# Causal attention in a Macaron block: masking inside VectorE's maximum instruction, whole-array maximum products in one even order, y turned a quad later

## What is computed

```python
def pair_attention_mask(t):
    m = jnp.tril(jnp.ones((t, t), dtype=bool))
    odd = jnp.arange(1, t, 2)
    return m.at[odd, odd - 1].set(False)
...
scores = jnp.einsum('bhqd,bhkd->bhqk', q, k) * scale
mask = pair_attention_mask(t)
scores = jnp.where(mask, scores, -jnp.inf)
w = jax.nn.softmax(scores, axis=-1)
y = jnp.einsum('bhqk,bhkd->bhqd', w, v)
```

## Time and profile before

| | us |
|---|---|
| median of 3 runs | 2261.66 (2257.74 to 2266.56) |
| the profiled execution | 2277.73 |
| its span, first to last instruction | 2275.9 |
| stage of the change in it | 1238 to 1818, 580 |
| busy in the span: PE, DVE, ACT, POOL | 1893.5, 1707.0, 1007.7, 799.4 |

### The profile page before, as it was taken

How to read it: one execution, slowest core, us unless ns; L and a number is a source line. 1 busy time by engine, 2 the same in 40 slices (tenths; PEclk the granted TensorE clock), 3 DMA queues, 4 the chain that set the end, 5 groups by cost and what they waited for, 6 DMA issues and landing times. The chain is left out here.

```text
span 2275.9 us, 37061 instructions
## 1 busy us (share of the span) xinstructions
PE 1893.5 (83%) x11875; PEld 1340.2 (59%) x11875; DVE 1707.0 (75%) x3526; ACT 1007.7 (44%) x1972; POOL 799.4 (35%) x862
## 2 busy tenths in 40 slices
PE   2799997799997369889797799999999874588898
PEld 1677787687775257778674233333333362477787
DVE  8789874688886666768887777777777366676688
ACT  1333435333334523335565355555555635233345
POOL 2223321233333667773346000000000036677733
PEclk9999997999998669999998799999999986699999
DMA  5000001000002512234347254353342016122246
GB/s 181 1 1 0 0 1 35 22 1 0 0 1 77 184 47 86 87 89 146 105 117 173 39 71 56 51 71 56 51 71 37 1 56 206 40 87 89 87 138 194
DMA packets 116656, 156.61 MB, mean 69 GB/s; under 512 B 20967, under 2 KB 85773, under 8 KB 115981
## 3 DMA queue, kind: packets, MB, share of 16 engines
q1 hardware_dynamic: 99840, 112.83, 21.4%
q0 software_dynamic: 14400, 40.41, 5.7%
q10 hardware_dynamic: 2252, 1.29, 0.2%
HBM read 107.00 MB, written 47.20 MB: 68 GB/s over the span
## 5 line engine op out<-in xcount | busy, mean ns | idle before, releaser
L2083 DVE TENSOR_REDUCE t_nm<-ps 128x1 f32<-128x512 f32 (+3 forms) x768 | 390.5, 552 | 102.3 <-PE ps L2173 50.7
L2149 ACT ACTIVATE t_E<-ps 128x1024 f32<-128x1024 f32 (+3 forms) x384 | 295.1, 808 | 244.4 <-PE ps L2201 191.1
L1569 PE MATMUL ps<-m_w,m_xT 128*128 (+1 forms) x1248 | 347.9, 414 | 10.3 <-DVE m_xT L1649 9.0
L1569 PEld LDWEIGHTS ps<-m_w,m_xT 128*128 128x128 f32 x1248 | 223.2, 192 | 53.2 <-issue 14.9
L693 PE MATMUL ps<-wdT,f_hT 128*128 128x256 f32 (+1 forms) x768 | 194.8, 396 | 18.2 <-ACT f_hT L735 18.2
L2198 PE MATMUL ps<-t_Qs,t_Ks 98*128 98x512 bf16 (+3 forms) x768 | 198.6, 339 | 5.0 <-DMA t_Qs<-t_mT 3.9
L1587 PE MATMUL ps<-m_w,m_hT 128*128 (+1 forms) x1248 | 201.5, 297 | 0.5 <-DVE m_hT L1666 0.5
L1656 DVE TENSOR_TENSOR m_ab<-ps,m_b 128x512 f32<-128x512 f32 x208 | 142.4, 685 | 68.5 <-PE ps L1569 45.2
L2068 POOL COPY t_Va<-t_V 128x128 f32<-128x128 f32 x64 | 16.1, 295 | 487.0 <-DVE t_mp L2094 486.8
L192 POOL TENSOR_TENSOR f_h<-f_h,f_hs 128x704 f32<-128x704 f32 x64 | 88.7, 1386 | 276.2 <-DVE f_h L230 276.2
L1621 ACT ACTIVATE m_hT<-ps 128x256 fp32r<-128x256 f32 x208 | 79.9, 384 | 223.5 <-PE ps L1578 135.2
(11 more groups left out here) (299 smaller groups left out, 3975.4 us busy)
## 6 DMA issues: line engine op xcount, KB each, us to landing
m_raw<-in_L_ffn_rw SPq DMA_DIRECT2D x48, 256.0 KB, 3.2
t_parts<-t_qkv_part SPq DMA_DIRECT2D x64, 192.0 KB, 2.8
t_Qs<-t_parts SPq DMA_DIRECT2D x96, 128.0 KB, 4.1
t_Ks<-t_parts SPq DMA_DIRECT2D x96, 128.0 KB, 6.7
m_yl<-m_picked_out SPq DMA_DIRECT2D x40, 256.0 KB, 2.9
m_rows<-m_xn SPq DMA_DIRECT2D x16, 512.0 KB, 4.2
m_xg<-m_rows SPq DMA_DIRECT2D x64, 128.0 KB
m_y<-m_picked_out SPq DMA_DIRECT2D x24, 256.0 KB, 3.1
```

The lines of the kernel that those rows point to most:

```text
L1569: last = nc.tensor.matmul(ps[:, H1 + u, :], xT[:, u, kx, k, :], of_expert(w1, kw, e, k), start=n == 0, stop=n == 3 * DC - 1)
L2083: nc.vector.tensor_reduce(dst, ps[:, bank, 0:n], AX_X, ALU.max, negate=True).then_inc(emptied, 1)
L2149: nc.scalar.activation(E[:, s % NPB, :, 0:n], ps[:, bank:bank + 2, 0:n], ACT.Exp, scale=float(HD) ** -0.5).then_inc(e_ok, 1)
```

## The change

- The maximum product is one for each head, on 96 rows of `Qs` and `Ks` from all six products of parts. `Qo` and `Ko` and their six transfers a quad go. The mask products at L2173 go.
- On the diagonal VectorE's instruction is `tensor_tensor_reduce`: it adds a bf16 row (`forbidden`: zeros, and the mask in the last 128 columns), multiplies by -1, takes the minimum into an accumulator, and writes the elementwise result to `unread`, which nothing reads.
- The 48 products go from large to small over the heads. `spread` places them over slots in proportion to the columns of TensorE's other work, without a break over the quads: those of quad q+1 end at slot 17 of quad q, and those of q+2 begin at slot 18. Each slot has two places, ahead of its scores and behind them. `nm` and `nm2` are double.
- `turn_max` for q+1 comes at slot 19 of quad q, y0 of q at slot 13. The last value products of a quad and its y1 come in the next quad, at slots 1 and 3.
- `y_ok` is dropped; ScalarE and SyncE wait for `pv_ok`.

```diff
--- before.py
+++ after.py
@@ -1921,49 +1921,85 @@
...
     QB = TPB
-    MAX_STEPS = [(pair, qb, k0, min(512, (qb + 1) * P - k0)) for pair in range(2) for qb in range(QB)
+    MAX_STEPS = [(h, qb, k0, min(512, (qb + 1) * P - k0)) for qb in reversed(range(QB)) for h in range(QUAD)
...
+    MAX_BY, M_AT, Y0_AT, Y1_AT = 18, 19, 13, 3
...
+    def columns(s):
+        Q, kb, _ = EXP_SLOTS[s]
+        n = 512 - max(0, kb - 4 * Q) * P
+        return 2 * n + (2 * P if kb >= 4 * Q else 0), (4 * n + 512 if s % 2 else 0)
+    def spread(slots):
+        places = [(s, i) for s in slots for i in range(2)]
+        work = [columns(s % NE)[i] for s, i in places]
+        share, at = sum(n for _, _, _, n in MAX_STEPS) / sum(work), {p: [] for p in places}
+        p, room = 0, work[0] * share
+        for k, (_, _, _, n) in enumerate(MAX_STEPS):
+            while room < n / 2 and p + 1 < len(places):
+                p += 1
+                room += work[p] * share
+            at[places[p]].append(k)
+            room -= n
+        return at
+    OF_FIRST, OF_REST = spread(range(MAX_BY)), spread(range(MAX_BY - NE, MAX_BY))
+    def max_steps(q, s, i):
+        steps = []
+        for j in (q + 1, q + 2):
+            if j < QUADS:
+                steps += [(j, k) for k in (OF_FIRST if j == 1 else OF_REST).get((s - (j - q - 1) * NE, i), ())]
...
+        at = {}
+        def put(*what):
+            at[what] = len(at)
+        for k in range(NM):
+            put(0, k)
+        put(0, "m")
+        for q in range(QUADS):
+            for s in range(NE):
+                for i in range(2):
+                    for j, k in max_steps(q, s, i):
+                        put(j, k)
+                if s == Y1_AT and q:
+                    put(q - 1, "y1")
+                if s == Y0_AT:
+                    put(q, "y0")
+                if s == M_AT and q + 1 < QUADS:
+                    put(q + 1, "m")
+        put(QUADS - 1, "y1")
+        return at
...
-            side, r = divmod(i - 2 * len(QPARTS), 3)
+            side, r = divmod(i, len(QPARTS))
             rows = scratch[side][q:q + 1, (QPARTS, KPARTS)[side][r], :, :]
-            odd = rows.rearrange("q (g o p) t -> p (q g) o t", o=2, p=HD)[:, :, 1, :]
-            sp.dma_start((Qo, Ko)[side][c][SECOND + r * HD:SECOND + (r + 1) * HD, :, :], odd).then_inc(stacked[c], 16)
+            sp.dma_start((Qs, Ks)[side][c][r * HD:(r + 1) * HD, :, :],
+                         rows.rearrange("q (h p) t -> p (q h) t", p=HD)).then_inc(stacked[c], 16)
...
         yT = ch.sb(name + "yT", [P, 512], ctx=until_y_done)
+        forbidden = ch.sb(name + "forbidden", [P, 512], BF16, ctx=until_y_done)
+        unread = ch.sb(name + "unread", [P, RING, 512], BF16, ctx=until_y_done)
...
                     if not end:
-                        sp.wait_ge(y_ok, q * 2 + 1)
+                        sp.wait_ge(pv_ok, q * NE + 4)
                         sp.sem_inc(ch.fence, 1)
                         stack(q + 2, (c + 2) % NQ)
...
-                        dst = (nm if k0 == 0 else nm2)[:, 2 * pair + i, qb:qb + 1]
+                    h, qb, k0, n = MAX_STEPS[k]
+                    at, bank = place(q, k)
+                    dve.wait_ge(filled, at + 1)
+                    dst = (nm if k0 == 0 else nm2)[:, q % 2, h, qb:qb + 1]
+                    if k0 + n == (qb + 1) * P:
+                        nc.vector.tensor_tensor_reduce(out=unread[:, bank, 0:n], in0=ps[:, bank, 0:n],
+                                                       in1=forbidden[:, 512 - n:512], scale=-1.0, scalar=-MASKED,
+                                                       op0=ALU.add, op1=ALU.min, accum_out=dst).then_inc(emptied, 1)
+                    else:
                         nc.vector.tensor_reduce(dst, ps[:, bank, 0:n], AX_X, ALU.max, negate=True
                                                 ).then_inc(emptied, 1)
-
-                def split_max():
+                    if k == NM - 1:
+                        split_max(q % 2)
...
+                nc.vector.memset(forbidden[:, :], 0.0)
+                nc.vector.drain()
+                nc.vector.tensor_copy(forbidden[:, 512 - P:512], ch.mask[:, 0, :])
+                nc.vector.drain()
...
-                    normalise(q, 1, end)
+                    for s in range(NE):
+                        for i in range(2):
+                            for j, k in max_steps(q, s, i):
+                                reduce_max(j, k)
+                        if s == Y1_AT and q:
+                            normalise(q - 1, 1)
+                        if s == Y0_AT:
+                            normalise(q, 0)
+                        if s == M_AT and not end:
+                            store_shift(q + 1)
                 turns(dve, step)
+                normalise(QUADS - 1, 1)
...
             def _(act):
-                def store_y(q, Q, end):
-                    act.wait_ge(y_ok, q * 2 + Q + 2)
-                    if Q or end:
-                        act.wait_ge(filled, place(q, "last y0" if end else "y0")[0] + (1 if Q else 0))
+                def store_y(q, Q):
+                    act.wait_ge(pv_ok, q * NE + 12 + 16 * Q)
+                    if Q:
+                        act.wait_ge(filled, place(q, "y0")[0] + 1)
                     elif q:
-                        act.wait_ge(filled, q * PER_QUAD + FIRST)
+                        act.wait_ge(filled, place(q - 1, "y1")[0] + 1)
                     nc.scalar.activation(yT[:, :], ps[:, YB, :], ACT.Copy).then_inc(y_stored, 1)
...
                                              scale=float(HD) ** -0.5).then_inc(e_ok, 1)
-                        if s == AT_Y:
-                            store_y(q, 0, end)
-                    store_y(q, 1, end)
+                        if s == 1 and q:
+                            store_y(q - 1, 1)
+                        if s == 9:
+                            store_y(q, 0)
                 turns(act, step)
+                store_y(QUADS - 1, 1)
...
+                def max_scores(q, k):
+                    h, qb, k0, n = MAX_STEPS[k]
...
-                    mine = [nc.tensor.matmul(ps[:, banks[0], 0:n], Qs[c][0:LEAD, 2 * pair, rows],
-                                             Ks[c][0:LEAD, 2 * pair, cols], start=True, stop=not diag),
-                            nc.tensor.matmul(ps[:, banks[1], 0:n], Qo[c][SECOND:SECOND + LEAD, pair, rows],
-                                             Ko[c][SECOND:SECOND + LEAD, pair, cols], start=True, stop=not diag)]
-                    if diag:
-                        mine = [nc.tensor.matmul(ps[:, bank, n - P:n], ch.identb[:, :], ch.mask[:, 0, :],
-                                                 start=False, stop=True) for bank in banks]
-                    mine[0].then_inc(filled, 1)
-                    mine[1].then_inc(filled, 1)
+                        pe.wait_ge(stacked[c], (q // NQ + 1) * LOADS)
+                    at, bank = place(q, k)
+                    if at >= RING:
+                        pe.wait_ge(emptied, at - RING + 1)
+                    nc.tensor.matmul(ps[:, bank, 0:n], Qs[c][0:STACK, h, qb * P:(qb + 1) * P],
+                                     Ks[c][0:STACK, h, k0:k0 + n], start=True, stop=True).then_inc(filled, 1)
...
                     last.then_inc(pv_ok, 2)
-                    if kb == 4 * Q + 3:
-                        pe.wait_ge(pv_ok, q * NE + 2 * k + 6)
-                        pe.sem_inc(y_ok, 1)
...
-
                     for s in range(NE):
-                        if not end:
-                            next_max(max_steps(s))
+                        for j, k in max_steps(q, s, 0):
+                            max_scores(j, k)
                         scores(q, c, s)
-                        if not end:
-                            next_max(max_steps(s, True))
-                        if s == LAST:
-                            turn_y(q, 0, end)
+                        for j, k in max_steps(q, s, 1):
+                            max_scores(j, k)
                         if s % 2 and s > 1:
                             values(q, c, (s - 3) // 2)
-                    if not end:
-                        turn_max(q)
-                    values(q, c, NE // 2 - 1)
-                    turn_y(q, 1, end)
+                        elif s == 1 and q:
+                            values(q - 1, (q - 1) % NQ, NE // 2 - 1)
+                        if s == Y1_AT and q:
+                            turn_y(q - 1, 1)
+                        if s == Y0_AT:
+                            turn_y(q, 0)
+                        if s == M_AT and not end:
+                            turn_max(q + 1)
                 turns(pe, step)
+                values(QUADS - 1, (QUADS - 1) % NQ, NE // 2 - 1)
+                turn_y(QUADS - 1, 1)
```

More of the change, by code:

```diff
@@ L1944, in causal_attention @@
     NPB = 4
     VW = HD + 1
-    AT_Y = 9
     NQ = 3
-    ROWS_OF_QUAD = 2 * (len(QPARTS) + 3)
+    ROWS_OF_QUAD = 2 * len(QPARTS)
```

(62 more changed lines are left out.)

55 lines of the change are left out of this document (12 added, 43 removed).

## The result

The changed kernel takes 2202.97 us (median of 4 runs, 2200.24 to 2205.28) where the kernel before takes 2262.87 beside it (2257.74 to 2266.56): a ratio of 0.9741 [0.9717, 0.9765], 60 us less. I had predicted 2216. The profiled execution after took 2202.50 us, with a span of 2200.7.

A forecast was written before the change was run, and what follows sets the result against it. TensorE was taken to bound the quad: 31.0 us instead of 33.58, 39 over 15 quads, plus 2 (last quad) and 5 (first), 46 off the profiled 2277.7: 2231.7; less 16.1 for the median, 2215.7. Range 2195 to 2275.

The forecast's parts named there:

- TensorE's floor, 29.7: TensorE alone would need 29.7 us a quad: 33.58 less 1.94 idle and 1.9 net saving.
- The price of a change of form: On TensorE, entering the 48-row form loses 0.09 us and leaving it 0.105.
- the entering term: TensorE saves some 16 enterings of the 48-row form behind whole-array work, 0.09 each: 1.4 us a quad.
- the leaving term: TensorE saves 24 leavings of the 48-row form, 0.105 each: 2.5 us a quad.
- The accumulator, 0.1 each: VectorE's new diagonal instruction costs 0.1 us more for its accumulator, 32 times: 3.2 a quad, VectorE's need 28.5.
- rival A: The accumulator is free and the banks hardly bind: 29.9 us a quad, time 2197; chance 0.15.
- Cluster waits, 1.2: TensorE waits for VectorE through the ring's three banks: 0.7 at slot 17, 0.5 elsewhere, 1.2 us a quad.
- B: Rival: VectorE becomes the bound, its accumulator read waiting 0.2 to 0.25 each; 2237 to 2263; chance 0.17.
- C: Rival: VectorE's diagonal instruction streams an element in two cycles, 10.7 us more a quad; 2355, near side 2311; chance 0.14.
- The clock's dips: Clock drops costing 2.7 us in each of three quads were assumed to stay, so no gain was counted.
- The first quad, 5 forecast: The first 48 reductions take 26.3 us instead of 31.3, with single products and 0.4 for preparing the mask row: 5 less.
- The last quad, 2 forecast: In the last quad TensorE's waits for the shift, 1.15, and the y, 0.81, both go: 2 us.

The follow-up runs named there:

- experiment 4: The changed kernel with each maximum product on the first 48 rows instead of 96, one at a time: 2313.59 us, ratio 1.0237.
- experiment 3: The kernel before with its paired 48-row products replaced by whole-array products on 96 rows, one after the other: 2260.43 us, ratio 1.0003.
- experiment 7: The changed kernel with one more short VectorE copy of 6 elements behind each diagonal instruction: 2214.9 us, ratio 0.9806.
- experiments 1, 2 and 5 to 9: Changed kernel with, respectively: TensorE masks; unmasked maxima; y at quad's end; TensorE masks and that y; extra VectorE copies; mixed product sizes; mixed, weighted: 2193.57 to 2235.21 us.

## Why the prediction was right, and where it was not

**The quad, 31.0 forecast and 31.00 measured, is right in the sum and less so in two terms, which offset each other.**
- TensorE's floor, 29.7: right. 31.00 less 1.5 of waits is 29.5. The price of a change of form, 0.09 to 0.105, was right (experiment 4), and with it the claim that TensorE gains though its columns double. By the trace the Trainium skill's statement (TensorEngine Tiling (Array Packing), Key Properties), that a change of tiling mode drains TensorE, holds, at about 0.095 us each. Taken alone, though, the whole-array products do not break even as 7.9 against 7.9: experiment 3 shows 0.57 more. Distances between starts, less 0.43 ns a column, tell where. Where maximum products stand behind scores, masks and y, what is left falls from 2.8 before to 1.8 in experiment 3, by 0.95 and not by the 1.4 of the entering term; the rest has come back as waiting for the banks. And the leaving term of 2.5 counted all 24 steps, but only 21 save it (2.2): the 3 ahead of value products have a change of form with either kind.
- The accumulator, 0.1 each: wrong, it is 0. The step took the row nearest to a short instruction, four aggregations at 0.38, and had "nothing" as its other end. The Trainium skill (VectorE: DVE Perf Modes, Two Vector instructions with no wait between them) says that such an instruction counts as two; the trace has the second, 83 ns, and no time for it. This part of rival A was true.
- Cluster waits, 1.2 (0.7 at slot 17 and 0.5 elsewhere): undersized. They are 1.5 with a VectorE that has 3.2 us less to do than I assumed, and 1.8 with experiment 7's load. The place was right: 1.0 at slot 17, behind the 256s and 128s, then 0.3 at slot 11 and 0.2 at slot 15. TensorE and then VectorE in order of time at slot 17:

```profile
1411.32 0.60 PE L2203 MATMUL ps<-t_Ks,t_Qs 96*128 96x256 bf16 x3
1412.12 0.79 PE L2203 MATMUL ps<-t_Ks,t_Qs 96*128 96x128 bf16 x3 [0.20 <-DVE t_nm L2106]
1412.84 1.06 PE L2243 MATMUL ps<-t_E,t_Va 128*32 128x512 f32 x8
```

```profile
1410.86 0.42 DVE L2106 CUSTOM_DVE_ANT_0 t_unread<-ps,t_forbidden 128x256 bf16<-128x256 f32 x1
...
1412.54 0.29 DVE L2106 CUSTOM_DVE_ANT_0 t_unread<-ps,t_forbidden 128x128 bf16<-128x128 f32 x1
```

  The six products before 1412.84, two of 256 and four of 128 columns, have 1,024 columns, 0.44 us, and take 1.5 (the first row counts one of the 128s with the 256s). The bracket of 0.20 is only the part in which no tail of a product runs. The forecast's time from the first of the eight products to the last, 2.1, is what was measured (1410.55 to 1412.68), but by luck. With free accumulators its five reductions make 1.7, not 2.1 (from 1410.86 to 1412.54, where the sixth starts); the rest is the 0.31 from the first product's start to its reduction and the 0.14 from the sixth reduction's start to the last product, which the forecast left out. And TensorE's own part was 1.2, not 1.4: the scores of slot 17 take 0.55 (1410.77 to 1411.32), not 0.9.

So rival A's 29.9 failed on the banks alone. B and C fell: VectorE is 85% busy in a quad (26.29 of 31.00) and the diagonal instruction streams like a reduction.

**The clock, the main miss.** "The clock's dips (2.7 in each of three quads) I leave as they are" was the step that failed. The kernel before loses 2.7 in each of three quads of the loop and has a fourth dip in the last; after has none in either of its profiles from the end of the first 41 us at half clock to the last y, nor has the one profile of each of experiments 1, 2 and 5 to 9, all with 96 rows, in the new order or mixed. In the table above that is 8.0 us of the loop, and the dip in the last quad is worth 2.2 more (experiment 3). I was too high by 13 us. 7 of them lie in the stage, which lost 53 where I had forecast 46: the loop's 8.0 and the first quad's 1.0 more than forecast, less 0.3 in the quads and 1.7 in the last piece. The other 6 lie outside the stage: the medians are 60 apart and the stages of the two profiled executions 53, and the median before, 2261.66 when I made the sum, is now 2262.87. Leaving the dips as they are was argued from nothing: the trace of before shows what a dip costs, not what brings it, and a change of the form of all maximum products could have been given a part of the range. Experiments 3 and 4 tie the dips to the 48-row products in either order, with the one dip of 3.4 us in experiment 3 as a remainder. Why they bring them isn't settled: the fewer rows, the gaps at the changes of form and the kinds of neighbours all go with them.

**The first quad, 5 forecast and 6.0 measured, is two errors.** The 48 reductions take 23.0 instead of 25.9, the accumulators again. But the first reduction starts 3.5 behind the block's start, not 1.6: the copy of the mask row, 128 columns of bf16, lasts 3.00 in the rows above where I gave the whole preparation 0.4. GpSimd fills the rows of `Ks` meanwhile:

```profile
1228.81 3.51 POOL L2024 MEMSET t_Ks<- 2x4096 bf16 x1 [3.92 <-POOLq L1737]
```

The fill ends at 1232.32 and the copy at 1232.37. In all ten profiles with this copy it ends 0.05 to 0.06 behind the fill, also in experiment 7, where it starts 0.4 later beside the fill and lasts only 2.63. So it looks as if the copy waits for the fill; no run moved the fill to prove it.

**The last quad, 2 forecast and 0.3 measured.** The piece isn't like for like, as L2123 now stands six slots earlier than L2094 did. Taken apart at the last quad's first scores, the two waits that I meant are indeed gone: 0.81 for y and 1.15 for the shift before, 0.19 after, so 1.8 less. The dip of the clock is 2.2 less. Against these stand 3.1 more of TensorE's work between L2123 and those scores, which lay ahead of L2094 before, and 0.6 more behind them, where the last values and the y of the quad before now come. The first of the 15 distances of the loop holds six slots less for the same reason, beside the end of the start's half clock, and so what the table has above the full-clock period does too; that share I have not separated. TensorE in order of time, after:

```profile
1729.22 0.39 PE L2226 MATMUL ps<-t_Qs,t_Ks 98*128 98x512 bf16 x1 [0.19 <-DMA t_Qs<-t_mT]
...
1738.43 0.61 PE L2226 MATMUL ps<-t_Qs,t_Ks 98*128 98x512 bf16 x2 [0.33 <-ACT t_E L2183]
...
1753.83 0.66 PE L2254 MATMUL ps<-ident,t_yT 128*128 128x128 f32 x4 [0.72 <-ACT t_yT L2175]
```

and before:

```profile
1801.08 0.60 PE L2198 MATMUL ps<-t_Qs,t_Ks 98*128 98x512 bf16 x2 [0.33 <-ACT t_E L2149]
...
1816.38 0.66 PE L2229 MATMUL ps<-ident,t_yT 128*128 128x128 f32 x4 [0.81 <-ACT t_yT L2141]
```

The last y of all waits for ScalarE's copy in both kernels, and so do the scores of the last quad for ScalarE's exponentials, where no maximum products are left. These waits are no part of the difference.

**Loads and y** were right: no load is waited for, and y0 and y1 are turned without idle in the loop.

**The size of each edit**, by the medians: order 25, mask on VectorE 21, y 14, whole-array products 0 alone (0.57 a quad and 2.4 in the first quad against the dips). By the stages of single profiles the first three are 25.6, 18.3 and 12.8. The prediction gave the whole-array products the largest term and the order none of its own.

## What to carry to other kernels

Price each change of TensorE's form from the distance between starts, count the places where it vanishes, and don't count those where a neighbour of another form keeps it. Where a faster engine meets a ring of few banks, part of what an edit removes comes back as waits (here 0.6 of 1.9), so price edits by the engine's floor plus the clusters, and look at order as an edit of its own: here it was the largest, and mixing large and small gave 9 us more. If the trace of before shows dips of the clock and the change alters what TensorE runs, their whole cost belongs in the range.

## What the runs showed of the hardware

- A VectorE instruction with an accumulator output leaves a second record, 83 ns, that overlaps the next instruction and moves no start (0.07 us a quad for 32 of them). A real copy of 6 elements at that place costs 0.16.
- A change between a 48-row product and whole-array work costs TensorE 0.09 to 0.10 us; 42 of them made a quad 3.75 us longer.
- With 48-row products among whole-array ones the clock fell to 1.2 GHz four times behind the start in the order of before, and in the new order stayed there for 167 us from the start and fell three times more. With 96-row products it fell once, for 3.4 us, in the order of before, and never in the new order or mixed, up to the last y. The cause is open.
- A copy of 128 x 128 bf16 on VectorE lasted 3.00 us at the start of the stage, beside a fill on GpSimd, and ended 0.05 to 0.06 behind that fill in all ten profiles. That it waits for the fill is likely, not shown by an experiment.
